# A fused tokenizer, retention and expert kernel: softmax sums taken from ones in the values' tiles, a new order of the work, expert turns written out

## What is computed

```python
p = exp(scores - max)
out = (p @ v) / p.sum(-1)
```

## Time and profile before

| | us |
|---|---|
| median of three runs | 1279.1 |
| the profiled execution | 1276.99 |
| its span, first to last instruction | 1275.0 |
| one turn of the main loop | 31.67 |
| main loop, to about | 975 |
| epilogue, to about | 1061 |
| experts, to the end | 1275 |

### The profile page before, as it was taken

One profiled execution on the slowest core, in us unless ns is written; L12 is line 12 of the kernel. 1 busy time (PEld: TensorE's weight loads), 2 busy tenths in 40 slices (PEclk: granted clock), 3 DMA queues, 4 the chain that ended last, 5 costly groups with the idle time before them and its releaser, 6 DMA issues.

```text
span 1275.0 us, 43269 instructions
## 1 busy us (share of the span) xinstructions
PE 1240.5 (97%) x15924; PEld 930.4 (73%) x15925; DVE 998.1 (78%) x2447; ACT 794.3 (62%) x1787; POOL 410.5 (32%) x268
## 2 busy tenths in 40 slices
PE   8999999999999999999999999999999876999998
PEld 6667777777777777777777777777776556999998
DVE  3678888888888888888888888888888766777776
ACT  2466666666666666666666666666666664556555
POOL 0000322232222222222222222222222146666666
PEclk9999999999999999999999999999999898999999
DMA  9522333333333333333333333333330013443332
GB/s 387 188 83 80 93 93 93 93 93 93 93 93 93 93 93 93 93 93 93 94 92 93 93 93 94 93 93 94 93 93 16 14 17 89 135 114 102 103 103 62
DMA packets 95146, 124.80 MB, mean 98 GB/s; under 512 B 56619, under 2 KB 77149, under 8 KB 94592
## 3 DMA queue, kind: packets, MB, share of 16 engines
q1 hardware_dynamic: 38400, 102.47, 25.4%
q0 software_dynamic: 56576, 19.93, 7.5%
HBM read 101.27 MB, written 20.82 MB: 96 GB/s over the span
## 4 chain that ended last, share of the span: by engine, by line
PE 80%; DVE 6%; issue 5%; DVEq 3%; POOL 2%; DMA 2%; ACT 1%; SPq 0%; POOLq 0%; ACTq 0%
PE bank_emb L479 22%; PE bank_s L550 10%; PE bank_x L564 7%; PE bank_y L460 7%; PE bank_s L637 4%; PE bank_s L614 4%; PE bank_z L460 4%; PE bank_y L649 3%; PE bank_y L667 3%; DVEq L1842 2%; PE bank_z L597 2%; DVE home_x L1846 2%; PE bank_s L460 2%; PE bank_y L690 1%; PE bank_s L843 1%
## 5 line engine op out<-in xcount | busy, mean ns | idle before, releaser
L1909 POOL DMA_INDIRECT expert_rows<-row_sb,placei x128 | 278.1, 2173 | 562.8 <-issue 464.8
L479 PE MATMUL bank_emb<-home_x 128*128 128x256 f32 x1216 | 338.1, 392 | 0.0
L479 PEld LDWEIGHTS bank_emb<-home_x 128*128 128x128 f32 x1216 | 210.3, 189 | 81.9 <-issue 56.5
L1374 DVE TENSOR_TENSOR home_s<-bank_s,con 97x776 f32<-97x776 f32 x256 | 239.3, 956 | 22.9 <-PE bank_s L550 22.8
L1926 POOL DMA_INDIRECT out_tokens<-yo,tok x104 | 122.9, 1181 | 69.7 <-issue 52.7
L1391 DVE TENSOR_REDUCE mx<-bank_s 97x8 f32<-97x776 f32 x128 | 117.7, 961 | 30.8 <-PE bank_s L614 30.6
L1102 ACT ACTIVATE home_s<-bank_s 97x776 f32<-97x776 f32 x128 | 97.5, 814 | 59.5 <-PE bank_s L637 59.5
L550 PE MATMUL bank_s<-qm,xn 32*97 32x452 f32 x1024 | 131.4, 580 | 1.7 <-DVE vp L1381 1.2
L564 PEld LDWEIGHTS bank_x<-home_s,vp 97*32 97x32 f32 x4096 | 90.0, 110 | 33.2 <-issue 29.4
L564 PE MATMUL bank_x<-home_s,vp 97*32 97x97 f32 x4096 | 111.8, 249 | 1.2 <-DVE vp L1381 1.2
L843 PE MATMUL bank_s<-w2e,home_s 128*128 x832 | 109.8, 275 | 0.0
(11 more groups left out here) (297 smaller groups left out, 2369.9 us busy)
## 6 DMA issues: line engine op xcount, KB each, us to landing
home_x<-in_x_main SPq DMA_DIRECT2D x96, 768.0 KB, 4.5
home_x<-expert_rows SPq DMA_DIRECT2D x104, 129.0 KB
w1e<-in_exp_w SPq DMA_DIRECT2D x1, 2576.0 KB, 13.2
txt<-in_txt_t SPq DMA_DIRECT2D x32, 64.0 KB, 3.6
w2e<-in_exp_w SPq DMA_DIRECT2D x1, 2048.0 KB, 17.6
expert_rows<-row_sb,placei POOLq DMA_INDIRECT x128, 8.7
out_tokens<-yo,tok POOLq DMA_INDIRECT x104
home_x<-in_x_tail SPq DMA_DIRECT2D x32, 48.0 KB, 3.4
```

The lines of the kernel that those rows point to most:

```text
L479: mm = pe.matmul(banks["emb"][:, 0:NPG], wtok[:, c, :], x_sb[:, c, :], start=(c == 0), stop=(c == KC - 1))
L1374: ins = dve.tensor_tensor(sm[:, k % 2, 2 * h:2 * h + 2, :], pair(h), decay, ALU.mult)
L1909: pool.indirect_dma_start(out=rows[:, :], out_offset=bass.IndirectOffsetOnAxis(ap=placei[:, k, c:c + 1], axis=0), in_=row_sb[:, k, c, E:E ...
```

## The change

Softmax sums: `b_sums` is gone. `vp2` is filled with ones instead of zeros, so that the 16 columns of a tile that hold no values give the sum. Even and odd heads can then no longer add up in one bank: `b_mixe` writes B.o (values of the even heads, sums beside them) and `b_mixo` writes B.den (values of the odd heads, sums beside them). The logs of both banks are taken with a scale and a bias per partition that turn the value rows into ln(1) = 0, added, and the 16-row halves of each 32 partitions are exchanged by a VectorE shuffle.

```diff
-            def b_sums(g, k):
...
-                        mm = pe.matmul(ps[32 * r:32 * r + 32, 2 * k * S:(2 * k + 2) * S],
-                                       const("den", S)[:, 32 * o:32 * o + 32], src, start=(o == 0), stop=(o == 1),
-                                       skip_group_check=True)
...
+            def b_mix(g, k, o, name):
...
                 for c in (2 * k, 2 * k + 1):
...
+                    j = 2 * (c % 2) + o
+                    for r in range(4):
+                        v = vp2[:, c, r, :, :].rearrange("p a b -> p (a b)")[:, 32 * o:32 * o + 32]
+                        mm = pe.matmul(ps[32 * r:32 * r + 32, c * S:(c + 1) * S], v, pt[:, k, r, j * S:(j + 1) * S],
+                                       start=True, stop=True, skip_group_check=True)
...
+            def b_mixe(g, k):
+                b_mix(g, k, 0, "B.o")
...
+            def b_mixo(g, k):
+                b_mix(g, k, 1, "B.den")
...
             def b_wo(g):
-                read(pe, g, "B.o")
+                pe.wait_ge(s_o2, g + 1)
```

```diff
-            def sums_log(g):
+            def sums_log(g, o):
+
+                ps = full(act, g, "B.den" if o else "B.o")
+                if g:
+                    act.wait_ge(s_swap, g)
+                act.activation(ln_sums[:, o, :], ps[:, 0:N], ACT.Ln, bias=const("odd" if o else "even"),
+                               scale=const("even" if o else "odd")).then_inc(s_lns, 1)
+
+            def odd_mix(g):
                 ps = full(act, g, "B.den")
-                drain(act.activation(rden[:], ps[:, 0:N], ACT.Ln), g, "B.den")
+                if g:
+                    full(act, g - 1, "B.wo")
+                drain(act.mul(o2[:], ps[:, 0:N], const("odd")), g, "B.den")
```

```diff
-            dve.memset(vp2[:], 0.0)
+            dve.memset(vp2[:], 1.0)
...
+            def sums_add(g):
+                dve.wait_ge(s_lns, 2 * g + 2)
+                dve.tensor_tensor(ln_sums[:, 0, :], ln_sums[:, 0, :], ln_sums[:, 1, :], ALU.add).then_inc(s_sums, 1)
+
+            def sums_swap(g):
+                dve.wait_ge(s_sums, g + 1)
+                if g:
+                    dve.wait_ge(s_o2, g)
+                dve.stream_shuffle(rden[:], ln_sums[:, 0, :], SWAP).then_inc(s_swap, 1)
+
+            def o_merge(g):
+                ps = full(dve, g, "B.o")
+                read(dve, g, "B.den")
+                drain(dve.scalar_tensor_tensor(out=o2[:], in0=ps[:, 0:N], scalar=const("even"), in1=o2[:], op0=ALU.mult,
+                                               op1=ALU.add), g, "B.o")
+
             def b_divide(g):
                 dve.wait_ge(s_rden, g + 1)
-                ps = full(dve, g, "B.o")
-                drain(dve.tensor_tensor(o2[:], ps[:, 0:N], rden[:], ALU.mult), g, "B.o")
+                read(dve, g, "B.o")
+                dve.tensor_tensor(o2[:], o2[:], rden[:], ALU.mult).then_inc(s_o2, 1)
```

New order: the loop runs to STEADY = NG - 1, part C has one turn more of lag, the banks are dealt anew, and all lists and the epilogue are new. PE's turn becomes:

```diff
+                at(a_scores, i - 1, 1, first=True)
+                at(c_rows, i - 4, 1)
+                at(b_center, i - 2)
+                at(ahead, i, 17, 19)
+                at(a_gate, i - 1)
+                at(a_scores, i - 1, 0)
+                at(b_var, i - 2)
+                at(ahead, i + 1, 0, 5)
+                at(b_shifted, i - 3, 0)
+                at(c_rank, i - 5)
+                at(ahead, i + 1, 5, 6)
+                at(b_q, i - 2)
+                at(a_mix, i - 1, 0)
                 at(a_scores, i - 1, 2)
+                at(b_k, i - 2)
+                at(ahead, i + 1, 6, 7)
+                at(b_mixo, i - 3, 0)
+                at(b_mixo, i - 3, 1)
                 at(a_mix, i - 1, 1)
                 at(a_scores, i - 1, 3)
+                at(a_mix, i - 1, 2)
+                at(b_mixe, i - 3, 0)
+                at(b_mixe, i - 3, 1)
+                at(ahead, i + 1, 7, 10)
+                at(b_scores, i - 2, 1, first=True)
                 at(a_center_ahead, i)
+                at(ahead, i + 1, 10, 13)
                 at(a_mix, i - 1, 3)
+                at(b_scores, i - 2, 0)
+                at(a_var_ahead, i)
+                at(ahead, i + 1, 13, 16)
+                at(b_values, i - 2)
+                at(b_max_t, i - 2, 1)
+                at(b_max_t, i - 2, 0)
+                at(a_yvar, i - 1)
+                at(b_wo, i - 3)
+                at(a_q_real, i)
                 at(a_q_imag, i)
+                at(b_shifted, i - 2, 1)
                 at(b_hrows, i - 2)
+                at(a_out, i - 1)
+                at(ahead, i + 1, 16, 17)
                 at(c_rows, i - 3, 0)
```

The part of DVE's turn around the new steps:

```diff
+                at(a_decayed, i - 1, 3, 1, last=True)
                 at(a_value_rows, i - 1, 3, 0, last=True)
+                at(sums_add, i - 3)
+                at(logit_shift, i - 4)
+                at(sums_swap, i - 3)
+                at(b_max, i - 2, 1, 1)
+                at(b_max, i - 2, 1, 0)
+                at(o_merge, i - 3)
+                at(top, i - 4)
                 at(a_low_ahead, i)
                 at(b_divide, i - 3)
```

In the epilogue PE has between the last mix and its `b_wo` nothing, as before only `c_rank`:

```diff
+            b_mixe(NG - 1, 0)
+            b_mixo(NG - 1, 0)
+            b_mixe(NG - 1, 1)
+            b_mixo(NG - 1, 1)
+            b_wo(NG - 1)
```

More of the change, by code:

```diff
@@ L89 @@
 KF = next(k for k in range(NG) if -(-(k * N - E * (P - 1)) // P) >= NT1)
-FIRST, LAST = -1, NG + 4
+FIRST, LAST = -1, NG + 5
 LAST_USES = [
[L92 to L107, removed]
-]
@@ L110 @@
+STEADY = NG - 1
+SWAP = [(i + DH) % 32 for i in range(32)]
 BANK_OF = {(g, use): bank for use, bank, _ in USES for g in range(NG)}
@@ L131, with counts @@
     take(_g, _use)
-def counts(order):
+def counts(order, last):
     seen, n = {}, 0
-    for i in range(FIRST, LAST):
+    for i in range(FIRST, STEADY):
         for *what, lag in order:
@@ L753, in _ @@
                 at(c_rows, i - 3, 0)
[L754 to L767, removed]
+            a_scores(NG - 2, 1, first=True)
@@ new lines, in _ @@
+            b_mixo(NG - 4, 0)
+            b_mixo(NG - 4, 1)
+            b_scores(NG - 3, 1, first=True)
+            a_center(NG - 1)
+            a_mix(NG - 2, 2)
+            a_mix(NG - 2, 3)
+            b_scores(NG - 3, 0)
+            b_hrows(NG - 3)
+            a_var(NG - 1)
+            b_max_t(NG - 3, 1)
+            b_max_t(NG - 3, 0)
+            b_values(NG - 3)
+            a_yvar(NG - 2)
+            b_wo(NG - 4)
+            a_q_real(NG - 1)
+            a_q_imag(NG - 1)
+            b_shifted(NG - 3, 1)
@@ L768, in _ @@
+            a_out(NG - 2)
+            c_rows(NG - 4, 0)
+            c_rows(NG - 4, 1)
+            a_scores(NG - 1, 1, first=True)
+            a_gate(NG - 1)
+            b_center(NG - 2)
+            a_scores(NG - 1, 0)
+            b_var(NG - 2)
+            c_rank(NG - 5)
+            b_shifted(NG - 3, 0)
+            b_k(NG - 2)
+            a_mix(NG - 1, 0)
+            a_scores(NG - 1, 2)
+            b_q(NG - 2)
             a_mix(NG - 1, 1)
-            b_q(NG - 2)
-            b_mix(NG - 3, 0)
+            b_mixe(NG - 3, 0)
@@ L865, in _ @@
             second_list()
-            with pe.Fori(2, TURNS1) as n:
+            for n in range(2, TURNS1):
                 turn(n)
             pe.wait_ge(s_list, 2)
-            with pe.Fori(TURNS1, TURNS - 1) as n:
-                turn(n)
-            turn(TURNS - 1, True)
+            for n in range(TURNS1, TURNS):
+                turn(n, n == TURNS - 1)
         @block.scalar
@@ L1242, in hidden @@
                                    bias=w1b[:, s, FF + f:FF + f + 1]).then_inc(s_gelu, 1)
-            for s in range(SLOTS):
-                hidden(0, s)
-            with act.Fori(1, TURNS) as n:
+            for n in range(TURNS):
                 for s in range(SLOTS):
@@ new lines, in _ @@
+            logit_max(NG - 5)
+            a_value_rows(NG - 2, 3, 0)
+            a_decayed(NG - 2, 3, 0, last=True)
+            a_decayed(NG - 2, 3, 1)
+            a_value_rows(NG - 2, 3, 1, last=True)
+            sums_add(NG - 4)
+            logit_shift(NG - 5)
+            sums_swap(NG - 4)
+            b_max(NG - 3, 1, 1)
+            b_max(NG - 3, 1, 0)
+            o_merge(NG - 4)
+            a_low(NG - 1)
+            b_max(NG - 3, 0, 0)
+            b_max(NG - 3, 0, 1)
+            y_low(NG - 2)
@@ L1878, in _ @@
             second_list_copy()
-            with dve.Fori(2, TURNS1 - 1) as n:
+            for n in range(2, TURNS1 - 1):
                 turn(n)
             dve.wait_ge(s_list, 2)
-            with dve.Fori(TURNS1 - 1, TURNS - 1) as n:
-                turn(n)
-            turn(TURNS - 1, True)
+            for n in range(TURNS1 - 1, TURNS):
+                turn(n, n == TURNS - 1)
             result(TURNS - 1, SLOTS - 1)
```

586 lines of the change are left out of this document (370 added, 216 removed), and 18 rows, old and new, of the table USES.

## The result

The changed kernel takes 1398.4 us (median of 4 runs, 1396.5 to 1401.7), the kernel before beside it 1279.0 (4 runs, 1277.0 to 1279.2): 1.094 times as long (95% interval 1.092 to 1.097), where 1247 was forecast. 119 us are lost where 32 were to be gained.

A forecast was written before the change was run, and what follows sets the result against it. PE's own queue was taken to bound the loop; sums -43.2, form changes +3, waits +3, epilogue +7, experts -2 give -32 us, from 1279.1 to 1247 us; range 1227 to 1267.

The forecast's parts named there:

- the paragraph on the experts: Experts' stage: written-out turns save 2 us; POOL's late scatter has over 20 us to spare.
- the one that ended slower: Loop: DVE's 5.5 us of idle time stays whole, turn 33.4 us, 1334 us in all; chance 0.06.
- the signs that I had named for being wrong: PE idle behind banks s0 to s3 in the loop; epilogue over 100 or under 80 us; experts longer than before.
- The turn: Main loop: PE needs 30.4 us per turn instead of 31.67; with waits 30.5 us.
- the slot of 1.35 us: PE: each group's 32 sum instructions leave the queue, 1.35 us per group, 43.2 us less over 32 groups.
- the 0.1 for one more change of form: PE in the loop: one more direct change between 32-row and 32-column products, 0.1 us per turn, 3 us more.
- The 0.1 of waits on DVE: Loop: PE waits for late maxima and what follows, 0.1 us per turn (0 to 0.6), 3 us more.
- the rival by the Trainium skill's rule: Loop: sums' slots filled by waiting for weights, PE only at 71%, turn stays near 31.5, 1279 us; chance 0.03.
- DVE's sum: Loop: add, merge and shuffle raise DVE's turn from 26.13 to 27.9 us (27.7 to 28.4).
- The epilogue: Behind the loop: exposed chains of the last groups and DVE's added work cost 7 us more (0 to 15).
- the epilogue eats more: Epilogue: deeper lag at DVE's pace and a second exposed chain, 16 us instead of 7, 1256 us; chance 0.12.
- The experts: Experts' stage: written-out turns save time at the loops' ends, 1 to 3 us, taken as 2 us less.

The follow-up runs named there:

- the kernel with four slots: The changed kernel with four row buffers (ROWS 3 to 4, yo laid over qm to make room); 1256.4 us, 0.984 of the kernel before.
- the first placing of the sums alone: The kernel before with its own order, lag and loops and only the new softmax sums, b_mixo standing where b_sums was; 1361.7 us.
- the one with the places earlier: The changed kernel, still three row buffers, with place_sum and place_index moved earlier on DVE in the loop; 1266.7 us, 0.992 of the kernel before.

## Why the prediction was wrong, step by step

**The step that failed** is a sentence in the paragraph on the experts: "POOL's `scatter` of a late group stands behind `text`, and its scattering (8.89 us per turn) has over 20 us to spare." It weighs POOL's load and so puts the wait for the scatter at nothing, but the load was never the matter; the wait and what followed from it cost 142 us. What counts is the time from the places to the landing (20.2 us, of which the four issues take 10.6 and the rest is landing and hand-overs) against the time until ACT wants the slot again. The diff told that part C lags one turn more and `ROWS` stays 3; I followed neither the tile nor `free_rows`. The trace of before had all the numbers (the last line is from its page: us from issue to landing):

```profile
412.53 0.14 DVE L1546 CAST placei<-placef 97x4 int32<-97x4 f32 x1
...
421.29 2.15 POOL L1909 DMA_INDIRECT expert_rows<-row_sb,placei  x1 [0.31 <-issue]
425.04 0.59 ACT L1120 COPY row_sb<-bank_y 97x512 f32<-97x512 f32 x1
...
expert_rows<-row_sb,placei POOLq DMA_INDIRECT x128, 8.7
```

The copy that needs this slot is one turn further, at 425.04 + 31.67 = 456.7, 44 us behind the places. A turn more of lag puts it at 425.04, 12.5 us behind them. By the page the last store lands at about 421.29 + 8.7 = 430.0, 17.5 us behind them; measured later, in the old order with two slots, it was 19.5 to the copy. A wait of 5 to 7 us per turn was there to be worked out; where in the turn the new order put the two steps made it 3.8. None of my rivals held this mechanism; the one that ended slower put the wait on DVE and the scores' banks, where the trace of after has none worth naming. Of the signs that I had named for being wrong only one came, a stretch behind the loop of more than 100 us (108.5), and it pointed elsewhere.

**The clock** was missing too: I priced no wait with what it does to PE's clock behind it. Per turn the wait was worth 3.6 us and the clock 1.6 more. Together 5.2 x 25 turns = 130 us, near the 134.4 by which the last projection starts later than with four slots (1079.1 - 944.7).

**The other steps**, read from the kernel with four slots, where nothing covers them:

- *The turn.* Forecast 30.4 to 30.6, measured 30.45. The sum of the slot of 1.35 us and the 0.1 for one more change of form holds; by itself neither was measured. The 0.1 of waits on DVE did not come. PE's busy time equals the turn, and its weight load is at 70% of it: the rival by the Trainium skill's rule ("Perfetto Trace Analysis", "Identifying the Most-Contended Engine") falls, since the turn shrank by about what left PE's queue.
- *DVE* 26.6 (forecast 27.9) and *ACT* 21.9 (22.0). DVE's sum came out 1.3 too high because durations don't simply add to busy time. Added up over one turn, DVE's durations grow from 29.0 to 30.7 us, by the 1.7 that the forecast had; but many an instruction starts before the one ahead of it has ended, and these overlaps, which busy time counts once, grow from 2.8 to 4.0 us. It decided nothing.
- *The shuffle* 0.585 us (forecast 0.56), with a mask load of 0.014. The estimate from the Trainium skill ("VectorE: DVE Perf Modes", perf-mode tiers) was 0.6; the trace agrees.

```profile
L1557 DVE STREAM_SHUFFLE rden<-ln_sums 128x388 f32<-128x388 f32 x32 | 18.7, 585 | 0.0
L1557 DVE LOAD_MASK_SELECT rden<-ln_sums x32 | 0.4, 14 | 0.1
```

- *The last group's wait* ahead of `b_wo`: forecast about 3 us, ended by DVE's divide; measured 3.17.

```profile
1033.18 1.66 PE L497 MATMUL bank_z<-o,woc 128*128 128x388 f32 x2 [3.17 <-DVE o L1568]
```

- *The epilogue* is the term of the wrong size. Forecast +7, less three groups' slots that lie there (3 x 1.35), so +3; measured +14.0 (85.6 to 99.6). With unread products in the gaps it is 90.5, so 9 of the 14 went with the clock, which the forecast didn't price. This was the rival "the epilogue eats more" (16 us, 1256). Its time is met by luck: it named the deeper lag, DVE's pace and a second exposed chain, but the old lag with the new sums has the same growth (85.6 to 99.8), and the clock isn't in it. What the other 5 us are was not tested apart.
- *The experts*: forecast -2, measured -3.4.

In spans, from the kernel before to four slots: -31.3 to the last projection, +14.0, -3.4, so -20.7 (1275.0 to 1254.4, with rounding), where the forecast was -32. Had `ROWS` been 4, 1247 would have been 9 us too low, and within the range.

## What to carry to other kernels

When a step of a hand-made pipeline gets a turn more of lag, list every tile that crosses it with its number of slots, and for each the time from the write that starts its last use to that use's landing, a DMA's too, against the time until the slot is wanted again; an engine's load says nothing about it. Here the wait that PE met in every turn was paid twice, once as idle time (3.6 us) and once as products at the lower clock behind it (1.6 us). Where the gap can't be closed, unread products in it can shorten the kernel.

## What was not expected of the hardware

Unread products made two kernels faster, by 27 us in the loop and 7.6 in the epilogue. ACT's log with a scale and a bias per partition takes 0.67 us for 128 x 388 from a bank, where the forecast took the 0.49 of the plain one; the multiply beside it takes 0.58:

```profile
L1183 ACT ACTIVATE ln_sums<-bank_y,con 128x388 f32<-128x388 f32 x31 | 20.7, 666 | 2.0 <-PE bank_y L690 2.0
...
L1190 ACT ACTIVATE o<-bank_y,con 128x388 f32<-128x388 f32 x31 | 18.0, 581 | 0.0
```

In the kernel after and in the one with four slots, the last of the four indirect stores of nearly every turn occupied POOL for 3.24 us instead of 2.15, and in the first placing of the sums alone the third took 3.4; in the loops of the kernel before and of the one with the places earlier all four took about 2.15. I have no cause for it.
